# Layer-norm and attention chain: the weights' parts of mlp1 made during the last attention batch, a cast and a mask row moved later in the opening, the context values evicted in two halves

## The reference

```python
x = L0(x, ctx, mask0)      # 32 query heads, 8 key heads of 8: softmax attention, residual, layer norm
x = L1(ctx, x, mask)       # 16 heads of 16; keys and values from x and ctx together (256 + 64), mask on the ctx part;
                           # residual, rms norm, then gelu(out @ mlp_w1 + b1) @ mlp_w2 + b2, plus residual
x = L2(x, ctx)             # one head: x + alpha * softmax(q k) v @ w_o
x = L3(x, ctx, ctx)        # two pre-norm attentions of 16 heads of 128, then a gelu MLP of width 1024
```

## Time and profile before

| what | before |
|---|---|
| three runs, us | 1135.31, 1135.68, 1128.23 |
| median, us | 1135.31 |
| profiled execution, us | 1139.85 |
| its span, us | 1138.1 |
| mean granted clock of TensorE | 0.974 |
| PE busy | 1055.4 us, 93% of the span |
| DVE busy | 728.5 us, 64% |
| ACT busy | 601.7 us, 53% |
| POOL busy | 452.7 us, 40% |

### The profile page before, as it was taken

One profiled execution on the slowest core, in us unless ns is written; L12 is line 12 of the kernel. 1 busy time (PEld: TensorE's weight loads), 2 busy tenths in 40 slices (PEclk: granted clock), 3 DMA queues, 4 the chain that ended last, 5 costly groups with the idle time before them and its releaser, 6 DMA issues.

```text
span 1138.1 us, 18506 instructions
## 1 busy us (share of the span) xinstructions
PE 1055.4 (93%) x6532; PEld 771.5 (68%) x6532; DVE 728.5 (64%) x1490; ACT 601.7 (53%) x1110; POOL 452.7 (40%) x436
## 2 busy tenths in 40 slices
PE   6889887699999987999989999999999999999998
PEld 3667765356665545677768876666788766667887
DVE  5777861656677735145568977667589786664553
ACT  3577764156666564256548752323487632245643
POOL 2777785523342023111214425333444244346241
PEclk9889998889999997999999999999999999999999
DMA  8010006766777121010012220000123100000000
GB/s 299 4 29 2 1 3 91 109 103 98 109 106 106 15 76 37 6 61 1 19 38 93 94 66 1 0 1 1 56 91 97 74 1 1 1 1 1 20 28 28
DMA packets 37152, 55.95 MB, mean 49 GB/s; under 512 B 12550, under 2 KB 29510, under 8 KB 34758
## 3 DMA queue, kind: packets, MB, share of 16 engines
q1 hardware_dynamic: 34998, 54.25, 21.4%
q10 hardware_dynamic: 2064, 0.52, 0.2%
HBM read 45.34 MB, written 9.18 MB: 48 GB/s over the span
## 4 chain that ended last, share of the span: by engine, by line
PE 71%; POOL 9%; DVE 6%; issue 6%; ACT 4%; DMA 1%; SPq 1%; POOLq 0%; ACTq 0%; DVEq 0%
PE ps L1180 9%; PE ps L900 8%; PE ps L1066 7%; PE ps L1159 7%; PE ps L970 5%; PE ps L851 4%; PE ps L1077 4%; PE ps L1087 4%; PE ps L752 4%; POOL p L2111 3%; PE ps L818 3%; PE ps L971 3%; PE ps L832 2%; ACT pT L1223 2%; PE ps L870 1%
## 5 line engine op out<-in xcount | busy, mean ns | idle before, releaser
L1223 ACT ACTIVATE pT<-ps 128x512 f32<-128x512 f32 (+1 forms) x144 | 74.1, 558 | 151.0 <-PE ps L1171 119.2
L1740 DVE TENSOR_REDUCE nm<-ps 128x1 f32<-128x320 f32 x256 | 114.4, 486 | 54.0 <-PE ps L818 51.2
L1180 PE MATMUL ps<-v,pT 128*128 128x256 f32 x512 | 118.8, 385 | 7.0 <-DVE xr L2006 3.7
L2296 POOL TENSOR_TENSOR pn<-p,sm 128x1024 f32<-128x1024 f32 x32 | 60.8, 1901 | 151.5 <-DVE sm L2001 151.5
L2237 POOL TENSOR_TENSOR wl<-bun_m,wh 128x512 fp32r<-128x512 f32 x64 | 80.5, 1261 | 100.5 <-ACT wh L1223 100.5
L1159 PE MATMUL ps<-g,cT 128*128 128x512 f32 x256 | 114.8, 592 | 0.0
L1180 PEld LDWEIGHTS ps<-v,pT 128*128 128x128 f32 x512 | 94.8, 190 | 25.4 <-ACT pT L1223 11.9
L970 PE MATMUL ps<-wb,hid_high 128*128 128x512 f32 x256 | 96.8, 416 | 0.0
L1226 ACT ACTIVATE pT<-ps 128x512 f32<-128x512 f32 x160 | 85.3, 607 | 15.5 <-PE ps L832 15.3
L1226 ACT ACTIVATE p<-p 128x1024 f32<-128x1024 f32 (+1 forms) x64 | 68.3, 1068 | 40.9 <-DVE p L1993 39.9
L818 PE MATMUL ps<-ks,qs 97*128 97x320 bf16 x256 | 71.8, 312 | 13.5 <-DVE nm L1740 7.9
(11 more groups left out here) (229 smaller groups left out, 2653.5 us busy)
## 6 DMA issues: line engine op xcount, KB each, us to landing
bun_m<-in_heads SPq DMA_DIRECT2D x32, 515.0 KB, 3.5
ks<-k_parts SPq DMA_DIRECT2D x48, 160.0 KB
qs<-q_parts SPq DMA_DIRECT2D x48, 128.0 KB
q_parts<-qp SPq DMA_DIRECT2D x8, 384.0 KB, 8.3
k_parts<-kp SPq DMA_DIRECT2D x8, 384.0 KB, 6.5
w<-in_w SPq DMA_DIRECT2D x2, 1024.0 KB, 4.8
xr<-in_x SPq DMA_DIRECT2D x1, 2048.0 KB, 15.9
out<-xr SPq DMA_DIRECT2D x16, 128.0 KB, 1.7
```

The source lines that it names most:

```text
L1180: last = mm(o, pT3[half][:, n, :], v3[:, bass.ds(i, 1), 4 * half + n, :], start=half == 0 and n == 0, stop=half == 1 and n == 3)
L1223: return nc.scalar.activation(o, x, ACT.Identity, bias=bias, scale=scale)
L1740: v.tensor_reduce(nm1[i % 2][:, t, h:h + 1], ps[:, u % 2, 0:KEYS1], X, ALU.max, negate=True).then_inc(D1t["maxima"].sem, 1)
```

## The change

- `pc`, the cast of the context keys on ACT, moves behind the exps of the first two units (`keys_ctx_high1`). POOL's wait for x and the row vectors moves ahead of the first bias. The mask row on DVE moves from batch 0 to batch 2.
- On ACT `own1(0, ...)` moves from behind the second heads copy of the last batch to behind the copies of its third unit.
- The context values get a semaphore step for each half, and DVE evicts the first half in the last batch of layer 0. Layer 1's first two score units wait for the first half alone.
- On DVE `wa_low` 0 moves behind the division of the last heads, and the four casts of the second weights follow `wa_low` 1. `hid_low` 0 comes ahead of the last residual and `hid_low` 1 ahead of `wa_low` 2 and 3. On POOL the low parts of the second weights move ahead of the last root. The casts get a semaphore of their own, since the squares, whose semaphore they continued, now come behind them.

```diff
--- before.py
+++ after.py
@@ -329,8 +329,8 @@
         dma_bun = [sem(f"loaded_heads_{t}") for t in range(BUNS)]
         dma_out = sem("stored_out")
 
-        ppe = Steps(sem, "prep_pe", ["k0", "v0", "v1"])
-        pdv = Steps(sem, "prep_dve", ["ones", "b0", "k0", "k0_rest", "v0", "m1", "v1"])
+        ppe = Steps(sem, "prep_pe", ["k0", "v0", "v1a", "v1b"])
+        pdv = Steps(sem, "prep_dve", ["ones", "b0", "k0", "k0_rest", "v0", "m1", "v1a", "v1b"])
         act_k0_rest = sem("l0_act_keys_rest")
         ppo = Steps(sem, "prep_pool", ["zeros"])
 
...
@@ -766,8 +766,8 @@
                             last = mm(ps[HALF * hf:HALF * (hf + 1), b // 2, (b % 2) * D:(b % 2 + 1) * D],
                                       cT[:, kt, b * SC:(b + 1) * SC], wt(w1, W1, "wv")[:, kt, :],
                                       start=kt == 0, stop=kt == KT - 1)
-                if half:
-                    last.then_inc(ppe.sem, ppe.did("v1"))
+                name = ("v1a", "v1b")[half]
+                last.then_inc(ppe.sem, ppe.did(name))
 
             for step, i, k in steps0("T1 N-2 S4 V1 H-1 S5 P-1 B0 B1 T2 S6 V2 N-1 T3 H0 S7 V3 P0 T4 Q2 B2 V4 B3"):
                 if step == "Q":
...
@@ -823,7 +823,7 @@
                 if p == 0:
                     pe.wait_ge(dma_max, 64 * (i + 1))
                     if i == 0:
-                        pe.wait_ge(pdv.sem, pdv.now(0, "v1"))
+                        pe.wait_ge(pdv.sem, pdv.now(0, "v1b"))
                 wait(A1["weights"], i, p - 3)
                 bank, q, k = 2 + (QUADS * PIECES * i + p) % 3, qs1[i % 3], ks1[i % 3]
                 if r < 4:
@@ -1241,6 +1241,8 @@
                 for mt in range(KT):
                     last = copy(tc1[:, mt, :], ps[:, 4 + mt, :], bias=pvec("L1_bk", mt))
                 last.then_inc(A1["k_ctx"].sem, 1)
+
+            def keys_ctx_high1():
                 wait(A1["k_ctx"], 0)
                 copy(pc1[:, 0, :, :], tc1[:, :, :]).then_inc(A1["k_ctx_high"].sem, 1)
 
@@ -1314,13 +1316,15 @@
                         keys_ctx1()
                 elif step == "C":
                     turned0(i, k)
+                    if i == B - 1 and k == 2:
+                        own1(0, "q", 0)
+                        own1(0, "k", 1)
                 elif step == "E":
                     weights0(i, k)
+                    if i == 0 and k == 1:
+                        keys_ctx_high1()
                 elif step == "O":
                     heads_out0(i, k)
-                    if i == B - 1 and k == 1:
-                        own1(0, "q", 0)
-                        own1(0, "k", 1)
                 elif step == "N":
                     normed_columns0(i, k)
                 elif step == "R":
@@ -1645,17 +1649,19 @@
             def mask_row0():
                 v.tensor_scalar(mask1[:, :], maski[:, :], 0.0, MASKED, ALU.is_equal, ALU.mult).then_inc(pdv.sem, pdv.did("m1"))
 
-            def values_ctx1():
-                dve.wait_ge(ppe.sem, ppe.now(0, "v1"))
+            def values_ctx1(half):
+                name = ("v1a", "v1b")[half]
+                dve.wait_ge(ppe.sem, ppe.now(0, name))
+                batches = slice(half * B // 2, (half + 1) * B // 2)
                 for e in range(2):
-                    heads = vc1[:, :, :, :].rearrange("p b (g e r) d -> p (b g) e r d", e=2, r=2)[:, :, e]
+                    heads = vc1[:, batches, :, :].rearrange("p b (g e r) d -> p (b g) e r d", e=2, r=2)[:, :, e]
                     v.tensor_scalar(heads[:, :, :, D1:D1 + 1],
-                                    const("half", e).unsqueeze(2).unsqueeze(3).broadcast_to([P, B * H1 // 4, 2, 1]),
+                                    const("half", e).unsqueeze(2).unsqueeze(3).broadcast_to([P, B * H1 // 8, 2, 1]),
                                     1.0, None, ALU.mult)
                     last = v.tensor_scalar(heads[:, :, :, 0:D1],
-                                           ps[:, 0:4, :].rearrange("p k (g e r d) -> p (k g) e r d", e=2, r=2, d=D1)[:, :, e],
+                                           ps[:, 2 * half:2 * half + 2, :].rearrange("p k (g e r d) -> p (k g) e r d", e=2, r=2, d=D1)[:, :, e],
                                            const("half", e), None, ALU.mult)
-                last.then_inc(pdv.sem, pdv.did("v1"))
+                last.then_inc(pdv.sem, pdv.did(name))
 
 
             def wait(t, i, k=0):
@@ -1721,11 +1727,13 @@
                     maxima0(i, k)
                     if i == 0 and k == 1:
                         values0()
-                    if i == 0 and k == 3:
+                    if i == 2 and k == 3:
                         dve.wait_ge(dma_mi, 16)
                         mask_row0()
                 elif step == "H":
                     heads0(i, k)
+                    if i == B - 1 and k == 1:
+                        values_ctx1(0)
                 elif step == "Y":
                     sums0(i, k)
                 elif step == "N":
@@ -1820,16 +1828,15 @@
                 f = slice(2 * n, 2 * n + 2)
                 v.tensor_copy(w["wb"][:, f, 0, :], w["raw_b"][:, f, :]).then_inc(DM[m]["wb_high"].sem, 1)
 
-            def mlp_rows(m, w, loaded):
-                if m == 0:
-                    dve.wait_ge(loaded, 32)
-                    for n in range(4):
-                        mlp_down_high(m, w, n)
+            def mlp_hidden_low(m, w, i, f):
+                wait(AM[m]["h_high"], i, f)
+                v.tensor_tensor(w["h"][1][:, f, :], w["hf"][f % 2][:, :], w["h"][0][:, f, :].bitcast(F32), ALU.subtract
+                                ).then_inc(DM[m]["h_low"].sem, 1)
+
+            def mlp_rows(m, w, done=0):
                 for i in range(NCH):
-                    for f in range(FT):
-                        wait(AM[m]["h_high"], i, f)
-                        v.tensor_tensor(w["h"][1][:, f, :], w["hf"][f % 2][:, :], w["h"][0][:, f, :].bitcast(F32), ALU.subtract
-                                        ).then_inc(DM[m]["h_low"].sem, 1)
+                    for f in range(0 if i else done, FT):
+                        mlp_hidden_low(m, w, i, f)
                         if m and i + 1 < NCH and 2 <= f < 2 + QC:
                             mlp_normed(i + 1, f - 2)
                         if m and i == 0 and f < QC:
@@ -1892,7 +1899,7 @@
                 wait(AH["ctx_high"], a)
                 v.tensor_tensor(cp3[1][:, :, :], cT[:, :, :], cp3[0][:, :, :].bitcast(F32), ALU.subtract).then_inc(DH["ctx_low"].sem, 1)
 
-            values_ctx1()
+            values_ctx1(1)
             dve.wait_ge(dma_rowv, 48)
             for n in SLOTS:
                 if n == SLOTS[1]:
@@ -1902,7 +1909,8 @@
                     if n == B and move == "b0":
                         dve.wait_ge(E1["heads"].sem, E1["heads"].end(B))
                         mlp_input_high(0, m1, 0)
-                        mlp_up_low(0, m1, 0)
+                    elif n == B and move == "j":
+                        mlp_hidden_low(0, m1, 0, 0)
                     if move == "U":
                         maxima1(i, k)
                     elif move in ("b0", "b1"):
@@ -1914,12 +1922,16 @@
                     elif move == "m":
                         maxima_low1(i)
                     if n == B and move == "b1":
+                        mlp_up_low(0, m1, 0)
                         mlp_up_low(0, m1, 1)
+                        for q in range(4):
+                            mlp_down_high(0, m1, q)
                     elif n == B and move == "r":
+                        mlp_hidden_low(0, m1, 0, 1)
                         mlp_up_low(0, m1, 2)
                         mlp_up_low(0, m1, 3)
 
-            mlp_rows(0, m1, dma_m1)
+            mlp_rows(0, m1, 2)
 
 
             for h in range(TAIL2):
...
@@ -2160,9 +2172,6 @@
                         keys_ctx1(i - 1)
                 elif step == "M":
                     shift0(i, k)
-                    if i == 0 and k == 1:
-                        pool.wait_ge(dma_x, 16)
-                        pool.wait_ge(dma_rowv, 48)
                     if i == B - 1 and k == 2:
                         settle(pool)
                         alone1(G1["rows"], 0, 0, g.memset(oz1[0:2 * H1, :], 1.0))
@@ -2181,6 +2190,9 @@
                 elif step == "G":
                     rows0(i, k)
                 elif step == "X":
+                    if i == k == 0:
+                        pool.wait_ge(dma_x, 16)
+                        pool.wait_ge(dma_rowv, 48)
                     bias0(i, k)
 
 
@@ -2188,7 +2200,7 @@
                 if i >= 2:
                     wait(E1["heads"], i - 2, QUADS - 1)
                 else:
-                    pool.wait_ge(pdv.sem, pdv.now(0, "v1"))
+                    pool.wait_ge(pdv.sem, pdv.now(0, "v1b"))
                 g.tensor_copy(vt1[i % 2][:, 2, :, 0:D1 + 1], vc1[:, i, :, :]).then_inc(G1["values"].sem, 1)
 
             def bias1(i):
@@ -2238,9 +2250,6 @@
                                 ).then_inc(GH["low"].sem, 1)
 
```

(5 more changed lines are left out.)

8 lines of the change are left out of this document (4 added, 4 removed).

## The result

The changed kernel took 1120.51 us (1119.15 to 1122.23), the kernel before, beside it, 1135.49 (1128.23 to 1137.67): a ratio of 0.986, 95% interval 0.983 to 0.990. Forecast: 1118.8, range 1112 to 1128. The profiled executions took 1119.64 and 1139.85 us, so the two traces stand 20.2 apart and the medians 15.0.

The account below looks back on a forecast made before the run. PE work, seven tenths of the chain, was taken to set the end. Gains of 3.3 + 5.1 + 8.1 = 16.5 bring the profiled 1139.85 to 1123.35; allowing for its 4.5 above the median gives 1118.8 us, range 1112 to 1128.

Parts of the forecast that it names:

- Opening: Start of layer 0, batch 1: POOL's wait, mask row and key cast moved, PE's scores earlier; gain 3.3 us.
- The -2.1: In the opening: mask row out of DVE's queue, so PE's batch 1 scores start at about 32.7 instead of 34.80.
- my +0.3: Cost of the mask row in batch 2, between maxima and normalisation: 0.3 us, at most 2.19 if POOL holds it.
- 3.0 for the clock: In the opening: another 3.0 us if PE's high clock holds from 34.80 to 42.66; half, 1.5, was taken.
- Layer 0 to layer 1: Last batch of layer 0: ACT's exp first; 2.4 us for the hole, 2.5 for the early projections' clock; gain 5.1.
- second path: Start of layer 1: batch 0's 32 score units need stack 0, in by about 200; units end at about 222.
- mlp1: Attention to mlp1: 5.5 us before the fifth up product, 2.6 for four up products at high clock; gain 8.1.
- The squares' wait: In mlp1: DVE's squares wait for POOL's last low part of the second weights; cost 0.6 us.
- Clock rival: PE stays at 1.2 GHz at all three places; gains 1.8, 2.4 and 5.5, 9.7 in all, 1125.6 us; chance 0.19.
- Stack rival: Stack 0's loads land at 203 and hold layer 1; second step gives 2.7, 14.1 in all, 1121.2 us; chance 0.10.
- Slower rival: Mask row delays batch 3's scores; three more low-clock batches at 6.9 us each give +4.2, 1139.5 us; chance 0.04.
- Baseline: The profiled execution of the kernel before, 1139.85 us, stands 4.5 above the three runs' median, 1135.31.

Follow-up runs that it names:

- c0: The changed kernel itself with nothing undone, the yardstick run beside three undoings: 1123.44 us, ratio 0.988 to the kernel before.
- d1: c2 plus useless products on PE filling the hole before the transposition, the wait itself kept: 1123.41 us, ratio 0.989.
- d3: Changed kernel with batch 2's K projection in front of stack 0's first scores instead of behind the eighth: 1119.5 us, ratio 0.985.
- c1: Changed kernel with its whole mlp1 part undone (casts, low parts of the down weights, hidden low parts): 1130.74 us, ratio 0.996.
- f2: Changed kernel with only the down weights' casts and low parts back behind the last normed rows, hidden low parts still moved: 1122.42 us, ratio 0.988.
- d4: Changed kernel with stack 0's q loads right behind the q store, stack 2's constant rows behind stack 1's loads: 1120.44 us, ratio 0.985.
- f4: Changed kernel with only the mask row back in batch 0, POOL's wait and ACT's cast still moved: 1125.46 us, ratio 0.991.
- c2: Changed kernel with ACT's evictions of the early projections in front of the exponentials again: 1127.72 us, ratio 0.992.
- f1: Changed kernel with the edits of d3 and d4 together: 1121.06 us, ratio 0.986.

## Why the prediction was right, and where not

The size came out: 16.5 us of gain forecast, 15.0 measured between the medians (1118.8 against 1120.5) and 20.2 between the traces. Each of the three places was priced somewhat too high. By the undoings, in medians: 1.8, 4.3 and 7.3, together 13.4 of the 13.6 measured beside them; I had 3.3, 5.1 and 8.1. That they add up so well is partly luck, since each median has an interval of 2.6 to 4.3 us either way.

- **Opening, -3.3.** Scores at 32.7: at 32.03 in the trace, with the start 0.7 earlier. Hole of under 2 us: 1.53. The -2.1 is right (2.05 in *a*). The mask row's own work is 0.7 to 0.8 us and not the 0.3 that I read from where the subtraction ended; the other 1.3 is GpSimd's lateness and the cast. What the row costs in batch 2 (my +0.3) wasn't separated. Half of the 3.0 for the clock, 1.5: the rest of *b* gave 1.4 between the traces, but that is luck. The clock did fall again in the changed kernel's opening, and where it didn't (c0) *b* was longer; the term drowns in a scatter of 2 to 4 us between executions of one opening.
- **Layer 0 to layer 1, -5.1.** The best of the three. The hole is gone, the sixteen products take 3.7 us, and the share of the clock is 2.5 as priced. The wait gives 1.9 in the changed kernel's trace and 2.7 in others at the first issue of stack 1's loads, where I had 2.4; the turn itself stands 2.6 us nearer to the first early projection (6.06 against 8.66 in d1). Stack 0 "in by about 200": it was in at 196.5 with the opening 4.2 sooner, 200.7. What I missed is that this makes the first scores wait 5.92 us; I called it a second path, and it is level with the first within the 0.35 us that d3 gave in *c*.
- **mlp1, -8.1.** Fifth up product: 5.5 priced, 5.1 found (it stood 7.47 us behind the turn, now 2.35). Four up products: -2.6 priced and -2.6 found between the two traces, -2.0 against c1. The squares' wait: 0.6 priced, 0.4 found. What I had wrong is the cause. "DVE makes the casts ahead of the first low part" is true, but the casts didn't have to move (f2): the two hidden low parts that go ahead of them were enough.
- **Clock rival, 0.19.** Wrong at two of three places. d1 shows for the second that TensorE's idleness in the hole of 2.43 us brought the low clock there. In the opening the clock did fall again, at about 33.5.
- **Stack rival, 0.10.** Half right: the wait is there, but taking the work behind it forward gained only 0.35 us in *c* before stack 1 set the pace (d3). With both stacks sooner *c* fell by 2.5 (d4).
- **Slower rival.** More batches at the low clock do occur, by 2.6 us each, with the same code; they moved single executions and not the verdict.
- **Baseline.** I took the profiled execution's 4.5 us above the median as a constant. It isn't one: the changed kernel's stands 0.9 below its median. That is why the traces show 20.2 us and the medians 15.0, and that the forecast of the median still came out is luck in part.

The port pair mattered three times: casts of 3.58 against 1.43 us, the square's 0.80 against 0.42, the mask row's 2.19 against 0.84. By the Trainium skill (SBUF — State Buffer, section "Who interferes with whom") casts and tensor_scalar may take the shared pair as well as instructions with two SBUF inputs, and whoever issues first keeps it. In these three the runs agree that one of the two is held; in f4 the mask row and the shift ran side by side and neither was (0.84 and 1.90 us). Which one isn't settled by who starts: in f2 GpSimd's first subtraction began 0.60 us behind the first cast (434.04) and the casts took 1.43 us, in the kernel before 0.59 behind it and they took 3.56.

## What to carry to other kernels

When a change moves two things in front of the same wait, undo each alone: here the edit with the name (the weights' parts) added nothing beside a small companion, two low parts made first. Undoing one of two shows only that it isn't needed beside the other. Price a hole in TensorE's work with the slow work that may stand behind it: the hole of 2.4 us cost 2.5 more in clock, while holes of 3.2 us elsewhere mostly cost none. And name the resource that stands level with the one you relieve: d3 filled the wait at the first scores and gained 0.35 us there before the next stack's loads set the pace.

## What the runs showed of the hardware

- Filling a hole with useless products, without shortening the wait, kept the granted clock at 1.00 instead of 0.55 (1.2 GHz for most of the stretch) and was worth 2.5 us in *c*. (By the ratios it was 3.6, with overlapping intervals.) A hole of 3.2 us before the turn of mlp1 left the clock at 1.00 in c2, d1 and f1.
- Where slot 0's first scores waited for stack 1's twelve loads of 128 and 160 KB (before, c2, d1, d3), they stood 16.80 to 17.15 us behind the first of them. In the other ten executions TensorE came 17.15 to 19.00 us behind it, without such a wait.
- The same instructions at the same places ran at clock 1.00 or 0.83 through whole batches, from one execution to the next: up to 4 us in *b* over the changed opening.
